# Layer norms' Newton steps moved from VectorE to GpSimd, and a bias product cut into four strips of 32 weight columns

## The reference

```python
def _layernorm(x, axis=-1, eps=1e-05):
    m = jnp.mean(x, axis=axis, keepdims=True)
    v = jnp.var(x, axis=axis, keepdims=True)
    return (x - m) / jnp.sqrt(v + eps)
...
    def _L0_attn_ref(...):
        ...
        scores = jnp.einsum('bhqd,bhkd->bhqk', q * scale, k)
        ...
        scores = scores + position_bias * 8.0
        attn = jax.nn.softmax(scores.astype(jnp.float32), axis=-1).astype(scores.dtype)
        ctx_out = jnp.einsum('bhqk,bhkd->bhqd', attn, v)
...
x = _layernorm(x + _L0_attn_ref(...), axis=-1)
x = _layernorm(x + _L0_ffn_ref(...), axis=-1)
```

## Time and profile before

| | us |
|---|---|
| Timed runs, median of 3 (lowest, highest) | 5642.71 (5641.98, 5645.2) |
| Profiled execution, its time | 5626.77 |
| Profiled execution, its span | 5625.0 |
| TensorE busy, of the span | 5183.8 |
| VectorE busy | 3972.7 |
| ScalarE busy | 2760.5 |
| GpSimd busy | 1340.1 |

### The profile page before, as it was taken

How to read it: one execution, slowest core, us unless ns; L and a number is a source line. 1 busy time by engine, 2 the same in 40 slices (tenths; PEclk the granted TensorE clock), 3 DMA queues, 4 the chain that set the end, 5 groups by cost and what they waited for, 6 DMA issues and landing times. The chain is left out here.

```text
span 5625.0 us, 103745 instructions
## 1 busy us (share of the span) xinstructions
PE 5183.8 (92%) x40013; PEld 2672.4 (48%) x40013; DVE 3972.7 (71%) x6826; ACT 2760.5 (49%) x4661; POOL 1340.1 (24%) x933
## 2 busy tenths in 40 slices
PE   6999997787999999998999979899999999997999
PEld 2333333444567777773333339433433434335676
DVE  7888886774567677777998944578688787864312
ACT  4767666221233333336786866454454454442333
POOL 0120100230112322322112214155344343440000
PEclk7999999787999999999999989999999999998999
DMA  4212110002111111111122113000000000001000
GB/s 91 49 33 32 33 32 12 0 0 63 37 33 25 30 26 30 26 30 31 27 39 38 42 51 88 29 20 17 13 13 20 9 13 13 13 16 35 5 5 8
DMA packets 148427, 158.08 MB, mean 28 GB/s; under 512 B 48980, under 2 KB 95108, under 8 KB 147508
## 3 DMA queue, kind: packets, MB, share of 16 engines
q1 hardware_dynamic: 143336, 142.37, 11.6%
q0 software_dynamic: 4096, 8.40, 0.5%
q10 hardware_dynamic: 504, 0.69, 0.1%
HBM read 118.20 MB, written 37.40 MB: 28 GB/s over the span
## 5 line engine op out<-in xcount | busy, mean ns | idle before, releaser
L4096 DVE TENSOR_REDUCE wide_max_parts<-wide_p 128x2 f32<-128x1024 f32 x496 | 595.2, 1220 | 130.0 <-PE wide_p L4065 117.9
L795 ACT ACTIVATE attn_w<-l_p 128x512 f32<-128x512 f32 x1024 | 553.4, 595 | 229.7 <-DVE l_p L1241 115.7
L2594 PE MATMUL caus_p<-caus_x_one,big 128*128 128x129 f32 x4608 | 634.1, 284 | 0.0
L641 DVE TENSOR_REDUCE l_max_parts<-l_p 128x2 f32<-128x1024 f32 x512 | 601.8, 1218 | 44.3 <-PE l_p L617 40.5
L2678 ACT ACTIVATE big<-caus_p 128x512 f32<-128x512 f32 (+3 forms) x768 | 345.9, 489 | 544.7 <-PE caus_p L2580 399.7
L641 DVE TENSOR_REDUCE rot_max_parts<-rot_p 128x2 f32<-128x1024 f32 x488 | 574.1, 1219 | 46.3 <-PE rot_p L617 43.1
L2594 PEld LDWEIGHTS caus_p<-caus_x_one,big 128*128 128x128 f32 x4608 | 585.1, 197 | 35.6 <-issue 2.3
L4373 PE MATMUL wide_p<-arena 64*128 64x512 f32 x2048 | 530.2, 596 | 0.0
L4511 ACT ACTIVATE attn_w<-wide_p 128x1024 f32<-128x1024 f32 x342 | 350.4, 1024 | 333.8 <-PE wide_p L4373 332.5
L4304 POOL TENSOR_TENSOR big<-big,attn_w 128x1024 f32<-128x1024 f32 x128 | 333.5, 2605 | 392.8 <-PE wide_p L4065 380.9
L641 DVE TENSOR_REDUCE caus_max_parts<-caus_p 128x2 f32<-128x1024 f32 (+2 forms) x360 | 340.4, 956 | 24.2 <-PE caus_p L617 15.9
(11 more groups left out here) (645 smaller groups left out, 9016.8 us busy)
## 6 DMA issues: line engine op xcount, KB each, us to landing
arena<-q_parts SPq DMA_DIRECT2D x576, 32.0 KB
arena<-k_parts SPq DMA_DIRECT2D x576, 32.0 KB
arena<-inverse_rows SPq DMA_DIRECT2D x64, 256.0 KB
l_q_stack<-q_parts SPq DMA_DIRECT2D x279, 32.0 KB
l_k_stack<-k_parts SPq DMA_DIRECT2D x279, 32.0 KB
q_parts<-arena SPq DMA_DIRECT2D x8, 768.0 KB, 3.7
k_parts<-arena SPq DMA_DIRECT2D x8, 768.0 KB, 3.6
attn_w<-moe_in SPq DMA_DIRECT2D x19, 256.0 KB
```

What stands on the lines that cost most here:

```text
L641: self.nc.vector.tensor_reduce(self.max_parts[:, 2 * p:2 * p + 2, n, half], pair[:, :, 0:self.width(n, half)], AX.X, ALU.max).then_inc(*se ...
L795: self.nc.scalar.activation(self.exps[t % len(self.exps)], bank, ACT.Exp).then_inc(*self.exped.up())
L2594: mm = nc.tensor.matmul(outs[o % 2][:, nq % 2 * (C + 1):(nq % 2 + 1) * (C + 1)], exps[h % 2][:, kb, nq * P:(nq + 1) * P], x_one[b % 2][:, ...
L4096: self.nc.vector.tensor_reduce(self.max_parts[:, :, n, h], side, AX.X, ALU.max).then_inc(*self.maxed.up())
```

## The change

**Near bias of the maxima.** Where a maxima tile of layer 0 touches the band, each of its two products with the flip matrix becomes four, one for each 32 columns of the weight, with the output on the 32 partitions that belong to them.

**Roots.** In the norms of `SideNorm`, VectorE makes the addition and the start (`start_on_dve`), and GpSimd the three Newton steps (`improve_on_pool`): one multiplication by -0.5, and four tensor_tensor a step with two constant tiles, since each has only two operands. At a set's first norm two memsets make the constants. That holds for three of layer 0's four norms, all four of the ternary rows' and three of the rotary layer's four; the last batch's norm in layer 0 and in the rotary layer stays with `root_on_dve`.

```diff
+    def start_on_dve(self, v, c):
...
+        v.wait_ge(*self.mv_done.at(NT * (c + 1)))
+        nc.vector.tensor_scalar(var[:, :], self.mv[:, :, 1], LN_EPS, None, ALU.add).then_inc(*rooted.up())
+        v.wait_ge(*rooted.now())
+        nc.vector.tensor_scalar(root[:, :].bitcast(bits), var[:, :].bitcast(bits), -0.5,
+                                float(ROOT_START), ALU.mult, ALU.add).then_inc(*rooted.up())
+
+    def improve_on_pool(self, pool, c):
...
+        if c == 0:
+            for tile, value in ((self.minus_half, -0.5), (self.three_halves, 1.5)):
+                nc.gpsimd.memset(tile[:, :], value).then_inc(*improved.up())
+        pool.wait_ge(*self.rooted.at(self.START * (c + 1)))
+        pool.wait_ge(*improved.now())
+        nc.gpsimd.tensor_tensor(var[:, :], var[:, :], self.minus_half[:, :], ALU.mult).then_inc(*improved.up())
+        for _ in range(ROOT_STEPS):
+            pool.wait_ge(*improved.now())
+            nc.gpsimd.tensor_tensor(square[:, :], root[:, :], root[:, :], ALU.mult).then_inc(*improved.up())
+            pool.wait_ge(*improved.now())
+            nc.gpsimd.tensor_tensor(square[:, :], square[:, :], var[:, :], ALU.mult).then_inc(*improved.up())
+            pool.wait_ge(*improved.now())
+            nc.gpsimd.tensor_tensor(square[:, :], square[:, :], self.three_halves[:, :],
+                                    ALU.add).then_inc(*improved.up())
+            pool.wait_ge(*improved.now())
+            nc.gpsimd.tensor_tensor(root[:, :], root[:, :], square[:, :], ALU.mult).then_inc(*improved.up())
...
     def centre_on_pool(self, pool, c, src, dst, part):
...
-            pool.wait_ge(*self.rooted.at(self.PER_ROOT * (c + 1)))
+            pool.wait_ge(*self.improved.now())
...
             for a in range(2):
-                mm = self.nc.tensor.matmul(pair[:, a, lo - half * BANK:hi - half * BANK],
-                                           self.core.flip_bf[:, :],
-                                           bias[:, 2 * p + a, lo - first:hi - first], start=False,
-                                           stop=True)
+                for at in range(0, P, PairWeighted.W):
+                    strip = slice(at, at + PairWeighted.W)
+                    mm = self.nc.tensor.matmul(pair[strip, a, lo - half * BANK:hi - half * BANK],
+                                               self.core.flip_bf[:, strip],
+                                               bias[:, 2 * p + a, lo - first:hi - first], start=False,
+                                               stop=True)
...
+                elif kind == "root" and args[0] + 1 < nb:
+                    norm.start_on_dve(v, args[0])
...
+                elif kind == "root" and args[0] + 1 < nb:
+                    norm.improve_on_pool(pool, args[0])
...
+        elif kind == "t_root":
+            self.norm.improve_on_pool(pool, n)
...
-            self.norm.root_on_dve(v, n)
+            self.norm.start_on_dve(v, n)
```

More of the change, by code:

```diff
@@ L217, with scale_on_dve @@
 class SideNorm(RootedNorm):
+    START = 2
+    def start_on_dve(self, v, c):
+        nc, rooted, var, root = self.nc, self.rooted, self.std, self.rstd
+        bits = mybir.dt.int32
+        v.wait_ge(*self.mv_done.at(NT * (c + 1)))
[4 more added lines that the diff above has]
+    def improve_on_pool(self, pool, c):
+        nc, improved, var, root, square = self.nc, self.improved, self.std, self.rstd, self.square
+        if c == 0:
[14 more added lines that the diff above has]
+            nc.gpsimd.tensor_tensor(root[:, :], root[:, :], square[:, :], ALU.mult).then_inc(*improved.up())
+    def scale_on_dve(self, v, c, src, dst, part=None):
+        if part != 1:
+            v.wait_ge(*self.rooted.now())
+        for i in range(NT) if part is None else range(part * NT // 2, (part + 1) * NT // 2):
+            self.nc.vector.tensor_scalar(dst[:, i, :], src[:, i, :], self.mv[:, i, 0:1],
+                                         self.rstd[:, i:i + 1], ALU.subtract,
+                                         ALU.mult).then_inc(*self.out_done.up())
     def centre_on_pool(self, pool, c, src, dst, part):
@@ L232, in __init__ @@
         super().__init__(st)
-        self.centred = st.sem("norm_centred")
+        self.centred, self.improved = st.sem("norm_centred"), st.sem("norm_improved")
+        self.minus_half, self.three_halves = st.sbuf("minus_half", [P, NT]), st.sbuf("three_halves", [P, NT])
 class Turn:
```

## The result

The changed kernel takes 5596.1 us in the median of six runs (5581.5 to 5607.9), the kernel before 5642.3 beside it. The ratio is 0.992, with a 95% interval of 0.9904 to 0.9935. The forecast was 5597, range 5584 to 5614. The profiled execution took 5581.5 us, span 5579.7, where the sum in its terms said 5581.

A forecast was written before the change was run, and what follows sets the result against it. TensorE was taken to set layer 0's pace, VectorE close behind. 23 + 23.5 - 0.4 is 46 us: 5581 in profiled terms, 5597 timed with the median 16 us higher; range 5584 to 5614.

The forecast's parts named there:

- Edit 1: Layer 0's near bias of the maxima in 32-column strips: 0.11 us less a slot on TensorE, 23 us in all.
- plain slots: 48 layer 0 slots of 2.65 us: VectorE leaves 0.03 us of room, so 0.07 each in the mean, 3.3 us.
- long slots: 181 layer 0 slots of 2.8 us or longer, VectorE room 0.29 us or more: 0.11 each, 19.9 us.
- Edit 2: Newton's steps of norms in layer 0 and the rotary layer moved from VectorE to GpSimd: 23.5 us saved.
- the deduction of 0.2 a root: VectorE keeps 0.40 us in a root slot, so 0.2 is lost at each of nine roots, 1.8 us.
- Clock saved: Of clock falls at three of layer 0's four other roots, one counted as saved: 1.6 us, bounds 0 to 5.
- the -0.4: Linear attention: GpSimd's centring ends at 1010.2, after TensorE's weight load at 1009.8; 0.4 us lost, bounds 0 and 8.
- the cover: Layer 0: 12.8 us free between GpSimd's last centring and TensorE's turn of the rows, hiding chains of 3.4 to 11.3 us.
- rival (d): GpSimd's small instructions are long: above 1.12 us apart TensorE waits at every turn; at 1.5, 5655 us; chance 0.02.
- (a): VectorE takes over in layer 0's long slots too: Edit 1 gives 12, time 5608 us; chance 0.17 together with (b).
- (b): Strip issue at 25 ns each sets TensorE's pace: Edit 1 gives 17 us, time 5603; chance 0.17 together with (a).
- (c): The pause on TensorE stays whatever the strip's width: Edit 1 gives nothing, time 5620 us; chance 0.07.

The follow-up runs named there:

- edit 2 alone: The changed kernel with the near-bias strips put back to full products, roots still on GpSimd: 5616.6 us, ratio 0.996 against the kernel before.
- the first experiment: The kernel before with only the near bias of the maxima in strips, all roots on VectorE: 5618.7 us, ratio 0.9963.
- the four and the six traces above: Rotary layer lengths: four traces with all roots on VectorE, 768.0 to 775.5 us; six with three on GpSimd and whole statistics, 762.4 to 766.3.

## Why the prediction was right, step by step

**Edit 1, forecast 23 us, measured 20.4.** Compared slot by slot with the kernel of edit 2 alone, over all of layer 0 and with clock falls left out, 194 slots are 0.09 to 0.11 us shorter, 19.9 us together, and 31 are 0.02 shorter, 0.5 together. The mechanism was as told: nothing at L658, all at the step to the exponentials, plain slots in turn (2.54 and 2.63; 2.54 and 2.62 were forecast). The term that was mis-sized is the long slots': 181 times 0.11. The step shrank by 0.10, and of the 194 slots 38 are plain ones, of 2.65 us or less, so 156 long ones gave 15.9 us where 19.9 stood. Another 15 slots above 2.8 us, twelve of 2.83 and three of 4.00, gave only 0.02 each: the prediction had 0.29 us of room for every slot of 2.8 or more, but there VectorE binds, as the shortened reductions showed. The 54 plain slots gave 4.2 us, 0.08 in the mean, where 3.3 stood. Of the two places named for the gain, the change from full to strip holds all of it, 0.094 us, and the load of the second full weight nothing: the two products start 93 ns apart as full ones and as strips. What an edit 1 without edit 2 would do (5619, expected of the first experiment) was right by luck and wrong by place: edit 1 alone gives back 4.2 us at the ternary roots, which the sum had not seen because both edits were costed together.

**Edit 2, forecast 23.5 us.** Three of its terms can be read alone. A root of layer 0's own: three slots of 3.40, 4.36 and 4.26 us before are 3.50, 3.40 and 3.29 now, 1.8 us, where 1.7 stood less 0.2 for VectorE's remaining 0.40. A ternary root: 6.0 us, where 5.9 stood. A rotary root, the third one: 1.8 us by the starts (slots of 4.35 and 3.99 against 3.29 and 3.24). Of the deduction of 0.2 a root something is there: with the reductions shortened the two slots of the first root are 0.13 and 0.05 us shorter. But the gain of a root is still 1.8, above the 1.5 that the sum left of it. Clock saved, forecast 1.6: of the 20.7 us that edit 2 alone brings in the 220 slots, 12.0 are the two roots under the split, and the slots of the other four roots give 1.8, 3.5, 1.8 and 1.7. The odd one holds a fall of the clock that is gone, 1.7 us, as forecast one of three. The rotary layer is 4.6 us shorter in the first pair of traces, where 5.1 stood, but its length before moves by 7.5 us between two traces. The means of the four and the six traces above are 7.0 us apart. Three waits of 1.8 us are 5.4 of that; the rest is not told apart from the clock.

**GpSimd.** Forecast was 0.2 us an instruction with 0.15 of wait behind it, 4.5 us a chain; measured are 0.20, 0.08 and 3.56. In linear attention 2.0 us were added for the scan; one instruction took 2.25 in place of 0.20, and the chain lasted 5.6. The Trainium skill (SBUF — State Buffer, Who interferes with whom) has a VectorE instruction with two SBUF inputs contend with a GpSimd instruction that reads SBUF, for a shared port that is locked. The rows agree, 2.25 us under a scan of 2.29 whose inputs both lie in SBUF, and a chain of thirteen pays this only once for a scan. The centring ended 51.8 us after the stage's start where 53.3 was the forecast (1010.2 less 956.9), and the turn waited 0.36 us for it. In the second trace of the changed kernel the turn starts 55.0 us after the stage's start and waits for no centring:

```profile
971.87 1.04 PE L286 MATMUL lin_small<-ident,x_tok 128*128 128x128 f32 x8
```

So the -0.4 stood for a wait of that size that is there in one execution and not in the other, and no length of the stage can show it.

**The step that failed** is the cover, "so 12.8 us are free and both bounds are hidden", and with it rival (d), whose threshold was 1.12 us from start to start. Both were read at layer 0's own norm and carried over to the ternary rows, where the split of q stands between chain and centring. There 4.5 us are free beyond a chain of 3.56, and TensorE would wait from (3.56 + 4.47)/13, that is 0.62 us from start to start. The upper bound given for an instruction, 0.87 us, was then not hidden. It did not matter, since the instructions came in at 0.28.

**The rivals.** (a) fell by the shortened reductions. (b) fell by the rows: eight strips of 192 columns pass in 0.17 us, 21 or 22 ns each in the mean, against an estimated 25 by the Trainium skill (TensorEngine Tiling (Array Packing), Instruction Overhead). That the number of strips does not set the pace at all is seen where the near bias of the exponentials moves only 64 columns, in the changed kernel:

```profile
113.31 0.26 PE L826 MATMUL l_p<-l_near,l_flip_bf 128*32 128x64 bf16 x12
113.39 0.39 PE L815 MATMUL l_p<-l_q_stack,l_k_stack 98*32 98x512 bf16 x4
```

Twelve strips pass in 0.09 us, 7 ns each. So the time goes with the columns moved, and a price of 25 ns for each strip does not hold here; the measurement decides. (c) fell: the pause before the exponentials is gone. The one before the strips stays, as forecast. (d) had the right shape and far too dear an instruction.

**The sum.** 38.1 us in the 220 slots, 1.9 before them and 0.9 behind stand for 42.0 of forecast in layer 0 (23, 6.8, 11.8 and 1.6, less 1.2 of the 1.8). The 1.9 is no more than the spread of that start between two traces of one kernel (1.0 and 2.0 us). The rotary layer stands for the rest. That the whole agreed to 1 us in the profiled execution is partly chance, because linear and causal attention alone move by 8 to 10 us between executions, against each other here.

## What to carry to other kernels

Before a change of tile shape on TensorE, ask which neighbour in the stream has that shape: a small product in the shape of what follows it can save the pause between them, while cutting it into pieces of another shape saved nothing here. A step moved to a slower engine is free only as far as the nearest reader of its result, and each place where it runs has to be looked at, because the queue behind it differs. A long program is best compared over stretches that start and end at the same instruction; stages with idle time spread by more than the effect sought.

## What the runs showed of the hardware

TensorE pays about 0.1 us when the column width of its products changes from 128 or 64 to 32 (93 or 94 ns from 128, for 192, 128 and 64 columns moved), and none between near-bias strips and exponentials of 32. Strips of 32 weight columns in different column groups pass at the rate of the columns moved: twelve in 0.25 us with 192 columns each, twelve in 0.09 with 64.

A GpSimd tensor_tensor on 128x8 takes 0.20 us, and a chain with a semaphore between each two runs at 0.28 us from start to start; on VectorE the same-sized steps stand at 0.20. Under VectorE's scan one such instruction took 2.25 us in one trace of the changed kernel and 2.09 in the other.

Two traces of one program differ by 1.0 us (changed) and 2.0 us (before) already in where the same slot of layer 0 starts, while the 220 slots behind it repeat to 0.1 and 1.1 us. Linear attention at a mean clock of 0.80 took 350.2 and 358.6 us in two executions. What sets its length, beyond where the clock's falls come, stays open.
